# A graph network on one core: TensorE's building loop unrolled to 64 steps, with float32 products of constants ahead of its address loads, and attention gains two tiles later

## What is computed

```python
h = jnp.maximum(_layernorm(x), 0.0)
x = x + _L0_gnn_ref(h, edge_index, ...)   # attention: softmax over each node's incoming edges
h = jnp.maximum(_layernorm(x), 0.0)
x = x + _L1_gnn_ref(h, weight, bias, src, dst)          # graph convolution
h = jnp.maximum(_layernorm(x), 0.0)
x = x + _L2_gnn_ref(h, edge_attr_64, ..., src, dst)     # message MLPs in both directions
h = jnp.maximum(_layernorm(x), 0.0)
x = x + _L3_gnn_ref(h, ..., src, dst, edge_type_4)      # four gated recurrent steps
...
# in the attention layer
scores = jnp.clip(jnp.sum(qk[dst] * qk[src], axis=-1) / 8.0, -5.0, 5.0)
e = jnp.exp(scores - seg_max[dst])
out = segment_sum(e / segment_sum(e, dst)[dst] * v[src], dst)
```

## Time and profile before

| | |
|---|---|
| median of 3 runs | 15204.44 us |
| profiled execution: time, span | 15192.86 us, 15191.1 us |
| TensorE busy (products) | 11428.2 us, 75% |
| VectorE / ScalarE / GpSimd busy | 6105.2 / 3551.5 / 4591.4 us |
| TensorE's granted clock over the span | 0.873 |
| building stage, 352 to 3650 us | 3298 us, TensorE busy 1874.87, VectorE 2553.84, clock 0.62 |
| attention stage, 3790 to 5112 us | 1322 us, TensorE busy 1217.64, clock 1.00 |

### The profile page before, as it was taken

The page is one execution under the profiler, slowest core; times in us unless marked ns, Lnnn a source line. Parts: engine busy times, 40 slices in busy tenths (PEclk is TensorE's granted clock), DMA queues, the critical chain, the costliest instruction groups (busy, mean ns, idle before and its releaser), DMA issues.

```text
span 15191.1 us, 282636 instructions
## 1 busy us (share of the span) xinstructions
PE 11428.2 (75%) x60408; PEld 6461.2 (43%) x60409; DVE 6105.2 (40%) x28511; ACT 3551.5 (23%) x9549; POOL 4591.4 (30%) x4343
## 2 busy tenths in 40 slices
PE   2555555555999776777776677677589999999999
PEld 2322332233222345555555555555464444444443
DVE  6777777776444423333333333333330000000000
ACT  0444444443222112222222222222210000000000
POOL 2000000000000028888888888888700000000000
PEclk8666665666999889999999999999869999999999
DMA  2323322322111353333333333333549889899898
GB/s 91 98 96 97 98 96 97 97 97 94 71 68 68 127 167 42 41 41 42 42 41 41 41 41 42 42 42 42 35 136 342 341 331 342 327 346 341 329 342 304
DMA packets 1120443, 2096.51 MB, mean 138 GB/s; under 512 B 372941, under 2 KB 982880, under 8 KB 1012496
## 3 DMA queue, kind: packets, MB, share of 16 engines
q1 hardware_dynamic: 823736, 1913.57, 35.7%
q0 software_dynamic: 295904, 174.34, 10.3%
HBM read 1630.27 MB, written 457.23 MB: 137 GB/s over the span
## 4 chain that ended last, share of the span: by engine, by line
PE 52%; issue 21%; DVE 11%; POOL 9%; ACT 2%; DMA 2%; DVEq 1%; SPq 1%; POOLq 0%; another core or an unknown queue 0%; ACTq 0%
PE ps L1464 15%; PE ps L1126 8%; PE ps L1469 8%; POOL G L488 5%; POOL reverse L811 3%; PE ps L1181 3%; DVE hots L1792 2%; PE ps L1172 2%; DVE hots L1790 2%; PE ps L1327 2%; PE ps L1316 2%; DVE hots L1791 2%; PE ps L1317 2%; PE ps L1330 2%; DVE weighed L1866 1%
## 5 line engine op out<-in xcount | busy, mean ns | idle before, releaser
L1126 PE MATMUL ps<-hots 128*128 128x392 f16 x4859 | 1884.8, 464 | 1438.8 <-issue 886.4
L811 POOL DMA_INDIRECT reverse<-SD,sidx x1660 | 2644.5, 1593 | 390.3 <-issue 371.9
L1464 PE MATMUL ps<-chunk,feat 128*128 128x512 f16 (+1 forms) x10192 | 2278.5, 375 | 14.4 <-DVE feat L2138 13.5
L841 ACT ACTIVATE stagebuf<-ps 128x392 f32 x3248 | 1472.9, 503 | 1887.8 <-PE ps L1129 1804.2
L488 POOL DMA_INDIRECT G<-h_table,idx x1660 | 1652.0, 995 | 493.6 <-issue 486.9
L1327 PE MATMUL ps<-MS,OH 128*128 128x128 f32 x3320 | 780.5, 319 | 1271.7 <-issue 835.9
L1992 DVE TENSOR_TENSOR acc<-acc,ps 128x132 f32 x1660 | 485.1, 292 | 3105.2 <-PE ps L1330 3052.2
L1790 DVE TENSOR_SCALAR hots<-count_lo,key_lo 128x128 f16<-128x128 f16 x4859 | 1212.8, 250 | 750.5 <-PE ps L1129 750.5
L1464 PEld LDWEIGHTS ps<-chunk,feat 128*128 128x128 bf16 x10192 | 943.0, 98 | 1342.7 <-issue 349.5
L1792 DVE TENSOR_SCALAR hots<-count_hi,key_hi 128x294 f16<-128x294 f16 x4859 | 1429.9, 294 | 0.0
L1126 PEld LDWEIGHTS ps<-hots 128*128 128x128 f16 x4859 | 496.2, 102 | 2095.5 <-issue 1688.1
(11 more groups left out here) (415 smaller groups left out, 15154.1 us busy)
## 6 DMA issues: line engine op xcount, KB each, us to landing
chunk<-adj SPq DMA_DIRECT2D x720, 1792.0 KB, 9.0
adj<-stagebuf SPq DMA_DIRECT2D x406, 784.0 KB, 5.3
chunkA<-adj SPq DMA_DIRECT2D x48, 1792.0 KB, 6.6
chunk<-adj SPq DMA_DIRECT2D x60, 1232.0 KB, 6.2
G<-in_edge SPq DMA_DIRECT2D x1660, 32.0 KB
G<-h_table,idx POOLq DMA_INDIRECT x1660
reverse<-SD,sidx POOLq DMA_INDIRECT x1660
reverse<-acc SPq DMA_DIRECT2D x4, 3225.0 KB, 20.0
```

The lines of the kernel that those rows point to most:

```text
L811: nc.gpsimd.indirect_dma_start(reverse[j % R], bass.IndirectOffsetOnAxis(sidx[:, j:j + 1], 0), SD[:, j % R, :], None, compute_op=ALU.add). ...
L841: nc.scalar.activation(stagebuf[:, bass.ds(held["word"][j] >> ENDBITS, SLEN)].rearrange("p (x c) -> p x c", c=BLK)[:, :, 0:2], bank[j % 8] ...
L1126: nc.tensor.matmul(ps[:, bass.ds(held["banks"][j] & 7 * 512, 2 * COMBS)], hots[:, j % BRING, 0:P], hots[:, j % BRING, P:P + 2 * COMBS], st ...
L1464: nc.tensor.matmul(bank[k % 2][:, 0:cols], feat[0][:, hi, 0:2, :].rearrange("p a d -> p (a d)"), columns(chunk4, i % DRING, m, cols), star ...
```

## The change

The loop of `count` is 64 steps long instead of 16. The eviction counts for 64 steps (16 words) are loaded once per pass; the 16 bank words still once per 16 steps. After each sixteenth step, ahead of the next load, TensorE issues eight float32 products of two constant tiles (`ident` and `earlier`, 128x120 outputs) into PSUM columns 392 to 511 of the bank just cleared, which nothing reads. In attention the gains follow the scores by 4 tiles (`LAG`) instead of 2, with rings of 6 and 4 slots instead of 4 and 3.

```diff
-SB, EB, WB, AB, ARING = 4, 4, 3, 2, 2
+SB, EB, WB, AB, ARING = 4, 6, 4, 2, 2
+LAG = 4
+SWEEP = 64
+WARM = 8
...
+            aside = ps[:, 2 * COMBS:8 * 512]
+            def busy(n, j):
+                at_ = held["banks"][j % STEPW] >> 12 & 7 * 512
+                for _ in range(n):
+                    nc.tensor.matmul(aside[:, bass.ds(at_, 512 - 2 * COMBS)], ident[:, :], earlier[:, 0:512 - 2 * COMBS],
+                                     start=False, stop=True, skip_group_check=True)
             def count(k, j, it):
                 if j == 0:
-                    held["free"] = words(0, k + BATCH - 1, 16 // BATCH, BATCH, VW + 8)
+                    held["free"] = words(0, k + BATCH - 1, SWEEP // BATCH, BATCH, VW + 8)
+                if j % STEPW == 0:
                     held["banks"] = words(32, k, STEPW, 1, 7 * 512 * 4097)
...
+                if j % STEPW == STEPW - 1:
+                    busy(WARM, j)
-            pipeline(pe, BSTEPS, 16, 0, lambda it, j: stage(BSTEPS, 16, it, j, 0, count))
+            pipeline(pe, BSTEPS, SWEEP, 0, lambda it, j: stage(BSTEPS, SWEEP, it, j, 0, count))
...
-            for i in range(NI + 3):
+            for i in range(NI + LAG + 1):
...
-                if not 2 <= i < NI + 2:
+                if not LAG <= i < NI + LAG:
                     continue
-                n, hi = divmod(i - 2, NB)
-                last = gain(i - 2)
+                n, hi = divmod(i - LAG, NB)
+                last = gain(i - LAG)
```

More of the change, by code:

```diff
@@ L1125, in count @@
                     pe.wait_ge(evicted, held["free"][j // BATCH] & 4095)
-                nc.tensor.matmul(ps[:, bass.ds(held["banks"][j] & 7 * 512, 2 * COMBS)], hots[:, j % BRING, 0:P],
+                nc.tensor.matmul(ps[:, bass.ds(held["banks"][j % STEPW] & 7 * 512, 2 * COMBS)], hots[:, j % BRING, 0:P],
                                  hots[:, j % BRING, P:P + 2 * COMBS],
                                  start=False, stop=True, skip_group_check=True)
-                nc.tensor.matmul(ps[:, bass.ds(held["banks"][j] >> 12, 1)], zero16[:, :], zero16[:, 0:1],
+                nc.tensor.matmul(ps[:, bass.ds(held["banks"][j % STEPW] >> 12, 1)], zero16[:, :], zero16[:, 0:1],
                                  start=True, stop=True, skip_group_check=True).then_inc(step_done, 1)
+                if j % STEPW == STEPW - 1:
+                    busy(WARM, j)
             nc.tensor.matmul(bank[0][:, 0:1], zero16[:, :], zero16[:, 0:1], start=True, stop=True, skip_group_check=True)
-            pipeline(pe, BSTEPS, 16, 0, lambda it, j: stage(BSTEPS, 16, it, j, 0, count))
+            pipeline(pe, BSTEPS, SWEEP, 0, lambda it, j: stage(BSTEPS, SWEEP, it, j, 0, count))
             pe.wait_ge(w_loaded, 32)
```

## The result

The changed kernel takes 14974.35 us (median of 4 runs, 14959.41 to 14981.28) against 15206.91 us: a ratio of 0.9846 (0.9829 to 0.9863), 232 us faster. The forecast was 14770 us, and 14690 to 14960 us for the range: the direction holds, and nearly half of the gain is missing.

A forecast was written before the change was run, and what follows sets the result against it. TensorE's own sequencer was taken as the building stage's bound. Building -310 us and attention -125 us made -435 us on 15192.86 us, 14758; with the median 11.6 us higher, 14770 us, range 14690 to 14960 us (8 in 10).

The forecast's parts named there:

- Bound now, TensorE's sequencer: Building stage: TensorE's own sequencer sets the pace, 10.96 us per group of 16 steps, neither the array nor VectorE.
- The seam at the loop's end: Last of four seams in 64 steps: 16 words instead of 4 (+0.11 us), products' address and issue (+0.33): 3.80 us.
- the 30 us allowed for the low clock: Building stage: a fifth of it at the low clock, taking the gain from 341 to 310 us.
- Seams inside the 64 steps: Three of four seams: one load and the branch gone, products' issue added, 2.19 us instead of 3.36 us.
- Clock: Building stage: mostly the high clock with the products, near 0.9, worth next to nothing inside the steps.
- The rival of a clock that pays: Building stage: steps at the array's pace, VectorE the bound, stage about 2554 us, total 14335 us; chance 0.02.
- The rival of a low clock: Building stage: the clock stays low, stage -170 us, attention -125 us, total 14910 us; chance 0.14.
- Load beside queued products: Building seams: a table load neither waits for queued products nor is slowed by them; 1.10 us.
- the rival of a held sequencer: Building seams: queue does not take 32 instructions or load waits, seam +1.2 to 1.8 us, total 15000 to 15080 us; chance 0.10.
- Larger body: Building loop: about four times the instructions, no cost.
- Stretching: Building stage: table loads stretched by 0.66 us each, five loads in 64 steps instead of eight, 3.3 us.
- Attention: Attention stage: 0.42 us off each of 298 periods, to 3.84 us, -125 us; bounds 0 and 135 us.

The follow-up runs named there:

- e1: The changed kernel with eviction counts copied once to a packed row in partition 96 and loaded as 16 neighbours: 14765.9 us, ratio 0.9724.
- e8: The kernel before with each store of the building stage made twice, the second into tables that nothing reads: 15697.59 us, ratio 1.0327.
- e2: The changed kernel without the eight products of constants: 14862.72 us, ratio 0.9787.
- e5: The changed kernel with the packed row of eviction counts and without the products of constants: 14684.27 us, ratio 0.9659.
- e3: The changed kernel with four strided eviction counts loaded per 16 steps instead of 16 once in 64: 15008.76 us, ratio 0.9884.
- e9: The changed kernel with a loop of 32 steps instead of 64, so the strided load has 8 words: 15022.84 us, ratio 0.988.
- e10: The changed kernel with packed row, no products of constants, and bank words loaded 32 at a time: 14730.61 us, ratio 0.9688.

## Why the prediction was right and wrong

- **Bound now, TensorE's sequencer.** Right. Undisturbed seams came out at 2.15 us for 2.19, branches at 0.208 us, and in e1 and e8 the total moved by what the loads did: in e1 the mean sum of the end seam's loads fell from 6.10 to 3.57 us, times 75 the 190 us; in e8 1.64 us per group times 304 is the 497 us.
- **The seam at the loop's end, "16 words instead of 4 (+0.11 us)": the step that failed.** I took the price of 16 words from the only 16-word row, the bank words, which are neighbours in partition 32. The 4-word row was the nearer one: its words have the stride and the partition of the new ones, and 0.99 us for 4 already meant 0.25 us a word, or 4 us for 16; the earlier trace rows had a second load of four words, neighbours in partition 0, at 999 ns. It is 3.80 us undisturbed, 2.70 us more than taken, in each of 75 ends: about 200 us. In 64 steps the trace has 7.64 us in the end seam where the sum had 5.12 (3.80 and two stretchings), 1.15 us more in the inner seams and 0.53 us less in the steps: +191, +87 and -40 us over the stage. Less the 30 us allowed for the low clock, that is about the 202 us that the stage is short. e1 takes out the first term and lands at 422 us off, where 435 were forecast; that it comes so close is in part luck, since the other terms nearly cancel. The rows of the kernel before held the bound from above that was missing for this load, 16/4 of 0.99 us. A strided word costs 0.234 us here, one of the 16 neighbours 0.07 us (1.10 us for all).
- **Seams inside the 64 steps.** Right at the high clock. On average they are 3.23 us where the sum had 2.85 (2.19 and 0.66). A load there is stretched by 0.84 us on average instead of 0.66, and 0.25 us more is the late first step at the low clock, whose undisturbed seams are 3.48 us.
- **Clock.** Right that the stage would be mostly at the high one and that this is worth next to nothing inside a step (0.01 us). The share at the low one was nearer a third (0.84) than a fifth ("near 0.9"; the trace has the clock at 1.00 in the seam at 642.2 us and at 0.50 from 894.5 to 896.5 us), and it cost 0.25 us in each of 228 inner seams, 57 us for the 30 allowed. The rival of a clock that pays is refuted by e2 and e5: without the products the clock is 0.63 and the kernel 92 and 94 us faster. The rival of a low clock had 14910 us, nearer to the measured time than the forecast, but not the cause: the clock of the stage was 0.84, where a low clock would have left the 0.62 of before.
- **Load beside queued products.** Right: 1106 ns at 642.5 us with 16 records of products under way, and seams of this kind took 2.15 us where the rival had 1.2 to 1.8 us more than 2.19, so the rival of a held sequencer is out. How many instructions TensorE's queue holds no run shows; this load stands behind the 32 of the products (16 weight loads, 16 records) in the program and started 0.3 us after the first of them. The rival's own sum was wrong besides: -340 + 304 x 1.2 to 1.8 us is +25 to +207 us and not "about 0 to -80", which gives 15105 to 15290 us with attention's 125 us, not 15000 to 15080.
- **Larger body.** Right, no cost: 208 ns at the median for the branch of the 64-step loop as for that of 16 steps.
- **Stretching.** That stores stretch the loads is shown by e8; the size per load was near (0.66 us; measured 0.84 us in the inner seams, 0.60 us in the end seams).
- **Attention.** Right: 3.84 us per period, TensorE full, 135 us for 125; that is the upper bound given, all periods and not only the 298 with a wait.
- **The range.** It left this term no width at all: a cost taken from a row of another layout had been written down as known. With 3.80 us for the load the forecast itself would have been some 14970 us, above the whole range; that this meets the measured time owes something to the same cancelling.

## What to carry to other kernels

Price a register load from SBUF by a row with the same engine, stride, partition and count, and not by the count alone. Here the strided words cost TensorE nearly as much each as a single one (0.234 and 0.30 us), and packing them into a row of their own before the loop paid. When an engine's sequencer paces a loop, look at the time from the start of one step to that of the next at both clock levels before paying for a higher clock. Where the nearest rows disagree (1.1 or 4 us for this load), let the range hold both.

## What the runs showed of the hardware

- Register loads by TensorE's sequencer from partition 0: 0.30 us for a single word (L515 of the kernel before, 301 ns at the median of 60) and 1.00 us for 4 neighbours (L507 of the kernel before, 997 ns at the least of 400, 1016 at the median). With a stride of 4 words, at the least: 0.99 us for 4 words (L1112 of the kernel before, L1115 of e3), 1.93 us for 8 (L1115 of e9), 3.80 us for 16 (L1115 of the changed kernel). VectorE loaded the 4 neighbours in 0.34 us (L507 of the kernel before, 344 ns at the median).
- Register loads by TensorE's sequencer from the other two partitions, all neighbours, at the least: 1.10 us for 16 words from partition 32 (L1112 of the kernel before), 1.27 to 1.28 us for 16 from partition 96 (L1115 of e10 and e1), 2.30 and 2.13 us for 32 from partition 32 (L1115 of e10, 2302 ns at 1665.2 us and 2140 at 1645.7 us).
- With a store from SBUF in flight, the load of 16 neighbours took up to 3740 ns in the kernel before (at 1487.2 us), 2.6 us more than its shortest, and that of the 16 strided words up to 7185 ns in the changed kernel (at 2908.5 us), 3.4 us more.
- One table load of the changed kernel started at 642.5 us, beside 16 records of float32 products that ran from 642.24 us for 2.04 us, and took 1106 ns; the shortest of all took 1102.
- Eight float32 128x120 products took 2.04 us in the changed kernel at the high clock (from 642.24 us) and 3.44 us at the low one (from 894.54 us; the mean clock from 894.5 to 897.8 us was 0.54).
- With the steps paced by TensorE's sequencer, four groups of 16 steps, from the weight load of the first to that of the sixteenth, took 25.08 us in e1 at a granted clock of 0.87 and 25.78 us in e5 at 0.63, 3% more.
